# Splitting an expert's second product into three passes already in the first half, with part of the split on VectorE and GpSimd

## What is computed

```python
gate_logits = x_flat @ gate_w.T
topk_vals, topk_idx = jax.lax.top_k(gate_logits, K)          # K = 2 of E = 8
topk_w = softmax(topk_vals)
for e in range(E):
    h = gelu(x_flat @ w1[e].T + b1[e])                        # "up": 128 -> 512
    y = h @ w2[e].T + b2[e]                                   # "down": 512 -> 128
    out = out + comb[:, e:e + 1] * y
```

## Time and profile before

| | us |
|---|---|
| median of 3 runs (lowest to highest) | 195.1 (194.87 to 195.27) |
| the profiled execution | 193.53 |
| its span, first to last instruction | 191.7 |
| PE busy in it | 173.8 |
| ACT busy | 116.5 |
| DVE busy | 99.8 |
| POOL busy | 76.2 |

### The profile page before, as it was taken

How to read it: one execution, slowest core, us unless ns; L and a number is a source line. 1 busy time by engine, 2 the same in 40 slices (tenths; PEclk the granted TensorE clock), 3 DMA queues, 4 the chain that set the end, 5 groups by cost and what they waited for, 6 DMA issues and landing times.

```text
span 191.7 us, 3184 instructions
## 1 busy us (share of the span) xinstructions
PE 173.8 (91%) x1255; PEld 116.1 (61%) x1255; DVE 99.8 (52%) x171; ACT 116.5 (61%) x174; POOL 76.2 (40%) x64
## 2 busy tenths in 40 slices
PE   0698799899898999998998999899999999999991
PEld 0198667476456654445463556366666888888880
DVE  0579433878084356566000700071528979966673
ACT  3533743127626632224986498635669999999980
POOL 8304419586402020002633263328632939333222
PEclk9975999999999999999999999999999999999999
DMA  6898000000000000480000000000000086000001
GB/s 153 269 350 359 14 0 3 0 0 0 3 3 2 0 2 0 154 280 10 0 0 3 0 0 0 5 0 0 0 0 3 6 265 227 2 0 0 3 0 55
DMA packets 5647, 10.41 MB, mean 54 GB/s; under 512 B 1264, under 2 KB 1648, under 8 KB 5376
## 3 DMA queue, kind: packets, MB, share of 16 engines
q1 hardware_dynamic: 5072, 10.06, 15.3%
q10 hardware_dynamic: 560, 0.15, 0.4%
HBM read 9.65 MB, written 0.56 MB: 53 GB/s over the span
## 4 chain that ended last, share of the span: by engine, by line
PE 74%; DVE 10%; issue 5%; ACT 4%; POOL 3%; DMA 2%; another core or an unknown queue 0%; DVEq 0%; POOLq 0%; ACTq 0%
PE PS L1063 10%; PE PS L1043 8%; PE PS L1047 7%; PE PS L1044 7%; PE PS L1071 4%; PE PS L1068 4%; PE PS L1069 4%; PE PS L916 4%; DVE nmx L621 3%; PE PS L929 3%; PE PS L798 3%; PE PS L1000 2%; PE PS L818 2%; DMA convw_sb<-convw 2%; PE PS L829 2%
## 5 line engine op out<-in xcount | busy, mean ns | idle before, releaser
L469 ACT ACTIVATE room<-PS,b_sb 128x512 f32<-128x512 f32 x64 | 43.5, 686 | 32.7 <-PE PS L1047 31.8
L323 POOL TENSOR_TENSOR x_sb<-x_sb,room 128x512 f32<-128x512 f32 x15 | 22.5, 1500 | 53.0 <-DVE room L709 53.0
L700 DVE TENSOR_TENSOR Gl<-room,Gh 128x512 fp32r<-128x512 f32 x32 | 29.0, 922 | 11.1 <-ACT Gh L418 10.8
L1043 PE MATMUL PS<-x2h,w1h 128*128 128x512 f32 x64 | 32.8, 512 | 2.2 <-ACT room L469 2.2
L1063 PE MATMUL PS<-room,w_sb 128*128 128x512 f32 x64 | 32.1, 593 | 0.0
L621 DVE TENSOR_REDUCE nmx<-PS 128x4 f32<-128x1024 f32 x16 | 19.4, 1225 | 12.1 <-PE PS L929 8.3
L1047 PE MATMUL PS<-x2l,w1h 128*128 128x512 f32 x64 | 25.3, 396 | 0.0
L1044 PE MATMUL PS<-x2h,w1l 128*128 128x512 f32 x64 | 25.3, 395 | 0.0
L640 DVE RECIPROCAL att<-PS 128x256 f32<-128x256 f32 x4 | 7.0, 1756 | 34.0 <-PE PS L1016 34.0
L315 POOL TENSOR_TENSOR pairs<-probs 128x512 f32<-128x512 f32 x12 | 15.0, 1271 | 16.2 <-ACT probs L459 16.2
L1043 PEld LDWEIGHTS PS<-x2h,w1h 128*128 128x128 f32 x64 | 12.0, 188 | 14.7 <-issue 10.9
(11 more groups left out here) (114 smaller groups left out, 254.9 us busy)
## 6 DMA issues: line engine op xcount, KB each, us to landing
room<-comb_rows SPq DMA_DIRECT2D x16, 256.0 KB, 5.2
w1raw<-w SPq DMA_DIRECT2D x8, 256.0 KB, 5.9
w_sb<-w SPq DMA_DIRECT2D x2, 1024.0 KB, 10.1
x_sb<-x SPq DMA_DIRECT2D x2, 256.0 KB, 3.6
out<-x_sb SPq DMA_DIRECT2D x2, 256.0 KB, 4.2
attw_sb<-attw SPq DMA_DIRECT2D x1, 320.0 KB, 6.4
cst<-consts SPq DMA_DIRECT2D x1, 228.5 KB, 5.3
convw_sb<-convw ACTq DMA_DIRECT2D x1, 80.0 KB, 3.6
```

Source lines behind the costliest of these rows:

```text
L323: nc.gpsimd.tensor_tensor(t2[:, cols(p)], t2[:, cols(p)], part[:, s, :], ALU.add).then_inc(acc_done, 1)
L469: nc.scalar.activation(G[:, n % GR, :], PS[:, U_BANK[n % 2], :], ACT.Gelu, bias=b1_sb[:, c:c + 1])\
L700: nc.vector.tensor_tensor(Gl[:, n % GR, :], G[:, n % GR, :], Gh[:, n % GR, :].bitcast(f32), ALU.subtract)\
L1043: mm(o, w1h[e][:, ms], x2h[:, cols(p)], start=True, stop=False)
```

## The change

The downs of the first half are plain only for its first three experts (n < 12) and split from n = 12 on (`SPLIT0` = 12). The high parts of the 20 gelus n = 12 to 31 are made on VectorE; the low parts of the odd ones are made on GpSimd and those of the even ones on VectorE. The second half is split as before, high parts on ScalarE, low parts on VectorE.

The weights are split earlier: `w2h` on ScalarE at n = 0 to 7, in the order of experts 3 to 7, 0, 1, 2, and `w2l` on GpSimd for experts 3 to 6 at n = 1 to 4 and for experts 7, 0, 1, 2 at n = 26, 27, 29, 31. Memory: `w2h` takes the place of the raw first weights; `Gh`, `Gl` and four `w2l` that of the first half's attention; the other four `w2l` that of `pairs`, so the one for expert 7 waits for the last sums (`sums_done` 8).

The lags change from 3 to a pattern of 4 or 5 and 2, so that four downs are issued together at n = 16, 20 and 24 and none at the other steps from 13 to 23. The units stand at n = 11, 15, 19, 23, four steps apart. `weigh` stands one step later in the first half (visit k at n = 4k + 9). `gelu(n)` waits for the low part of n - 4 where that is split, as the buffer is free only then.

```diff
+W2_ORDER = [3, 4, 5, 6, 7, 0, 1, 2]
...
-        LAGS = [1] * 9 + [2] + [3] * (MT * VISITS - 10)
+        LAGS = [1] * 9 + [2, 3, 4, 2, 3, 4] + [5, 2, 3, 4] * 2 + [5, 2] + [3] * (MT * VISITS - 25)
...
-        WEIGH_LAG = 8
+        WEIGH_LAG = 9
...
-        SCORES, ATTENDS = {11: 4, 14: 5, 19: 6, 22: 7}, {16: 2, 24: 3}
+        SCORES, ATTENDS = {11: 4, 15: 5, 19: 6, 23: 7}, {16: 2, 24: 3}
...
-        SPLIT0 = MT * E
-        HIGH_W2 = {26: 0, 27: 1, 29: 2, 30: 3, 31: 4, 33: 5, 34: 6, 35: 7}
-        LOW_W2 = {27: 0, 28: 1, 30: 2, 31: 3, 37: 4, 39: 5, 41: 6, 43: 7}
+        SPLIT0, SECOND = 3 * MT, MT * E
+        HIGH_W2 = {n: e for n, e in enumerate(W2_ORDER)}
+        LOW_W2 = {**{n + 1: e for n, e in enumerate(W2_ORDER[:4])}, 26: 7, 27: 0, 29: 1, 31: 2}
+
+        def high_engine(n):
+            return "dve" if n < SECOND else "act"
+
+        def low_engine(n):
+            return "pool" if n < SECOND and n % 2 else "dve"
...
         def downs(n):
-            lag = [LAGS[k] - (k - 1 in SCORES) for k in (n - 1, n) if k >= 0]
-            done = [max(0, k + 1 - l) for k, l in zip((n - 1, n)[-len(lag):], lag)]
-            return range(done[0] if n else 0, done[-1])
+            return range(max(0, n - LAGS[n - 1]) if n else 0, n + 1 - LAGS[n])
...
-                if n == MT * k + WEIGH_LAG + (k == E) - (k > E):
+                if n == MT * k + WEIGH_LAG - 2 * (k > E):
...
+                if e == W2_ORDER[4]:
+                    pool.wait_ge(sums_done, 8)
...
+            def low_gelu(n):
+                pool.wait_ge(g_high["dve"], high_count(n))
+                nc.gpsimd.tensor_tensor(Gl[:, n % GR, :], G[:, n % GR, :], Gh[:, n % GR, :].bitcast(f32), ALU.subtract)\
+                    .then_inc(g_low["pool"], 1)
...
+                if n >= SPLIT0 and low_engine(n) == "pool":
+                    low_gelu(n)
...
+                if k >= SPLIT0:
+                    act.wait_ge(g_low[low_engine(k)], low_count(k))
...
+            def high_gelu(n):
+                dve.wait_ge(gelu_done, n + 1)
...
+                if n >= SPLIT0 + GR:
+                    dve.wait_ge(down_done, n - GR + 1)
+                nc.vector.tensor_copy(Gh[:, n % GR, :], G[:, n % GR, :]).then_inc(g_high["dve"], 1)
...
+                if SPLIT0 <= n < SECOND:
+                    high_gelu(n)
+                if n >= SPLIT0 and low_engine(n) == "dve":
                     low_gelu(n)
```

More of the change, by code:

```diff
@@ L69, in hybrid_program @@
         b1_sb = sb("b1_sb", [128, E * MT])
-        w1raw = [sb(f"w1raw{e}", [128, HID]) for e in range(E)]
+        with ExitStack() as early:
+            w1raw = [early.enter_context(nc.sbuf_tensor(f"w1raw{e}", [128, HID], f32)) for e in range(E)]
+        w2h = [sb(f"w2h{e}", [128, HID], f32r) for e in range(E)]
         w1h = [sb(f"w1h{e}", [128, HID], f32r) for e in range(E)]
@@ L114, in hybrid_program @@
         att = sb("att", [128, 2, TOK])
-        with ExitStack() as early:
[L117 to L128, removed]
+        kT = [sb(f"kT{g}", [128, T]) for g in range(2)]
+        qT = [sb(f"qT{g}", [128, T]) for g in range(2)]
+        other_nmx = sb("other_nmx", [128, 2, TILES, 128])
+        other_vpad = sb("other_vpad", [128, TILES, HEADS, 32])
+        shared_probs = sb("shared_probs", [128, 2, 4, 2, TOK])
+        with ExitStack() as early:
+            pairs = early.enter_context(nc.sbuf_tensor("pairs", [128, 2, 4, TOK], f32))
+        w2l = {e: sb(f"w2l{e}", [128, HID], f32r) for e in W2_ORDER[4:]}
+        with ExitStack() as early:
+            first_probs = early.enter_context(nc.sbuf_tensor("first_probs", [128, 2, 4, 2, TOK], f32))
+            first_nmx = early.enter_context(nc.sbuf_tensor("first_nmx", [128, 2, TILES, 128], f32))
+            first_vpad = early.enter_context(nc.sbuf_tensor("first_vpad", [128, TILES, HEADS, 32], f32))
         Gh = sb("Gh", [128, GR, HALF], f32r)
         Gl = sb("Gl", [128, GR, HALF], f32r)
+        w2l.update({e: sb(f"w2l{e}", [128, HID], f32r) for e in W2_ORDER[:4]})
+        nmx, vpad = (first_nmx, other_nmx), (first_vpad, other_vpad)
         PS = ctx.enter_context(nc.psum_tensor("PS", [128, 8, 512], f32))
@@ L287, in _ @@
             nc.gpsimd.memset(euler[:, :], float(np.exp(1.0))).then_inc(powers, 1)
-            nc.gpsimd.memset(vpad[:, :, :, :], 0.0).then_inc(vzero, 1)
-            nc.gpsimd.memset(nmx[:, :, :, :], 0.0).then_inc(vzero, 1)
+            for p in range(NHALF):
+                nc.gpsimd.memset(vpad[p][:, :, :, :], 0.0).then_inc(vzero, 1)
+                nc.gpsimd.memset(nmx[p][:, :, :, :], 0.0).then_inc(vzero, 1)
             for q in range(WQ):
@@ L362, in _ @@
                     low_weights2(LOW_W2[n])
-                if n >= WEIGH_LAG and n % MT == 0:
-                    k = (n - WEIGH_LAG) // MT
-                    accumulate(k, k % 2, k // E)
+                for k in range(VISITS - 2):
+                    if n == MT * k + WEIGH_LAG - (k >= E):
+                        accumulate(k, k % 2, k // E)
+                if n >= SPLIT0 and low_engine(n) == "pool":
+                    low_gelu(n)
             accumulate(VISITS - 2, 0, 1)
@@ L999, in values @@
                     for j in range(4):
-                        last = mm(PS[head_rows(j), PV_BANK[b], 0:TOK], vpad[:, 2 * b + mt, 2 * j + g, :],
-                                  probs[:, u % 4, j, mt, :], start=(g == 0 and mt == 0), stop=(g == 1 and mt == 1),
+                        last = mm(PS[head_rows(j), PV_BANK[b], 0:TOK], vpad[b // 2][:, 2 * (b % 2) + mt, 2 * j + g, :],
+                                  probs_of(u)[:, j, mt, :], start=(g == 0 and mt == 0), stop=(g == 1 and mt == 1),
                                   skip_group_check=True)
@@ L1012, in sums @@
                     pe.wait_ge(t2_ready, b)
+                    pe.wait_ge(prob_ready, 4 * b + 4)
                 for mt in range(1 if PAIRED[u] else 2):
                     for j in range(4):
[L1015 removed]
+                        addend = pairs[:, u % 2, j, :] if PAIRED[u] else probs_of(u)[:, j, mt, :]
                         last = mm(PS[head_rows(j), SUM_BANK[b], 0:TOK], ones_par[:, g, :], addend,
```

65 lines of the change are left out of this document (40 added, 25 removed).

## The result

| | before | after |
|---|---|---|
| median of the runs, us | 194.99 (194.04 to 195.27, 4 runs) | 200.26 (198.71 to 200.74, 4 runs) |
| ratio, with 95% interval | | 1.028 (1.022 to 1.034) |
| profiled execution, us | 193.53 | 200.74 |
| its span, us; mean granted clock | 191.7; 0.982 | 199.0; 0.966 |

The change costs 5.3 us. The forecast was 199.5, with a range of 194.0 to 202.5. Some executions of a kernel are slow ones, over 1.5% above its fastest: medians take them in and ratios leave them out, so the two disagree for `e3_both` and `e10_reduce_copy`, and the profiles of `e8_act24` and `e11_gate_first` are of slow ones.

A forecast was written before the change was run, and what follows sets the result against it. TensorE bounds from 150 us; earlier it also waits for gelus. With GpSimd and VectorE taking turns, +4.4 on the profiled 193.5 gave 197.9, and 1.6 for the median 199.5 us; own range 197.0 to 202.0, with other cases 194.0 to 202.5.

The forecast's parts named there:

- The mechanism and the sign: GpSimd and VectorE exclude each other by turns, making the norm's spread late; slower by 4.4 us.
- The turns: A GpSimd instruction takes 1.58 us alternating with a copy, 1.73 with a subtraction, against 1.28.
- From the spread to n = 35: up(30) starts 5.2 us late, less 0.9 by shorter downs; up(35) 4.4 late.
- The gate's transposes: TensorE's wait there stays, accumulate 6 and the exponential following low part 31: 0.
- Behind n = 36: Behind up(35) everything is as before, 1.39 us a step.
- casts do not wait for GpSimd: Nine copies in GpSimd's busy stretches save 0.3 us each: +1.7, 196.8 us; chance 0.15.
- faster, turns cost little: GpSimd goes at 1.28 us an instruction, up(35) starts at 141.8: -2.1, 193.0 us; chance 0.15.
- TensorE alone bounds: Fewer passes save 3.4 us and filled waits 3.2: -6.6, 188.5 us; chance 0.05.
- Worse: Casts of n = 13 to 15 held, a raw maximum delayed: +1.3 and +1 on top, 201.8 us; chance 0.10.

The follow-up runs named there:

- e3_both: Changed kernel with the last norm's variances and power moved ahead and w2l of experts 0, 1, 2 made at n = 33, 37, 41; 202.99 us, ratio 1.024.
- e10_reduce_copy: Changed kernel with VectorE's high parts written by a maximum over one element instead of a copy; 197.74 us, ratio 1.018.
- e8_act24: Changed kernel with high parts of n = 24 to 31 on ScalarE and their low parts all on VectorE; 197.31 us, ratio 1.011.
- e11_gate_first: `e9_all` with the second half's gate ahead of other work and the twelve high parts left on VectorE made by reduction; 193.35 us, ratio 0.995.
- e1_norm_first: Changed kernel with the last norm's variances ahead of high part 28 and their power ahead of w2l 0 and low part 27; 199.19 us, ratio 1.020.
- e5_order_only: Changed kernel with the first half's downs plain as before, keeping its lags, units and positions; 194.41 us, ratio 0.997.
- e9_all: Changed kernel, high parts from n = 24 on ScalarE, norm early, two accumulates late, w2l 0, 1, 2 at n = 29, 31, 35; 198.07 us, ratio 1.015.
- e12_order_gate: `e5_order_only` with the second half's gate ahead of weigh and low parts, its exponential one step sooner; 193.18 us, ratio 0.991.
- e4_before_memsets: Kernel before with GpSimd's two memsets cut into four of half the size; 195.0 us, ratio 1.000.

## Why the prediction was right, and where not

Two lines of VectorE in the profile after, the norm's `x2l` and a low part ahead of the gate, are read below:

```profile
143.31 1.66 DVE L698 TENSOR_TENSOR x2l<-xn,x2h 128x512 fp32r<-128x512 f32 x1
...
149.22 1.84 DVE L752 TENSOR_TENSOR Gl<-room,Gh 128x512 fp32r<-128x512 f32 x1
```

- *The mechanism and the sign* held. VectorE's high parts average 0.95 us (0.8 to 1.2 was said), the longest wait stands ahead of the spread with 3.45 (3 to 5 was said), and a step of up and split down in the first half takes 1.40 (111.73 to 113.13). `e1_norm_first` moves the norm ahead and shortens that wait to 0.46, `e8_act24` and `e10_reduce_copy` take away part of the load and shorten it to 1.80 and 2.35; `e5_order_only` takes all of the load away and the wait with it. Of GpSimd I had said over 1.5 on average and under 10 us idle from 109 to 148; it has 1.47 and 10.0.
- *The turns* were mis-sized. The five GpSimd instructions from accumulate 4 to low part 27 took 7.33 us (131.44 to 138.77), 1.47 each, where I had 8.3. All four groups together have 1.47 (30.9 us for 21), against 1.58 beside copies and 1.73 beside subtractions; why a turn costs less than the whole of the other instruction is not shown. In the burst before it the nine instructions took 14.60 (111.51 to 126.11) where I had 15.6, and that with an idle of 1.29 that I had at nothing. So the `up` behind the products of attend 3 starts at 127.69, with the 2.14 taken off 125.55, as before and not 1.1 later. The spread is +3.2 against before instead of +5.2.
- *From the spread to n = 35* the lateness was to fall from 5.2 to 4.4. It grew, from 3.2 to 3.7. From up(30) to up(35) the trace has 8.79 where I had 7.5. I had given the norm's own split nothing. Behind the spread `x2h` and `x2l` (1.66 us, before 0.69) now stand in turn with GpSimd, so `x2l` ends 4.4 us behind the spread's start (before: 2.9), and TensorE waits 0.57 for it. Counted by starts of passes that is 0.7 of the 1.3; the rest is TensorE's own work, for which 7.5 was too little. Of the low parts of this burst TensorE waits for none.
- *The gate's transposes* were the term that was wrong in kind. I wrote that the wait there "stays: 0". It rose from 0.40 to 1.81, of which 1.0 is net loss at the transposes. I had looked at GpSimd's exponential alone and not at VectorE, which has the indices and the gap behind a low part of 1.84 us, in turn with an accumulate. `e9_all` has the same fault at 2.6, and `e11_gate_first` and `e12_order_gate` remove it.
- *Behind n = 36* I had 0 and the trace has 0.4: 26 steps at 1.40 instead of 1.387. Its cause is open, but it is not of the split downs: `e5_order_only` and `e12_order_gate` have 1.40 too, and `e4_before_memsets` has 1.387. The early clock, +2.14, was in no term either; it is not of the change, as variants of the changed kernel have their first `up` at 61.84 (`e10_reduce_copy`) and 62.17 (`e5_order_only`).

So the forecast came out near for a reason that is partly luck. It was 2.0 too dear up to the spread, 1.3 too cheap from there to up(35), and 1.4 too cheap at the gate and behind; the errors nearly cancel, and the last product stands at +5.1 where +4.4 was forecast. The medians differ by 5.3. The rival "casts do not wait for GpSimd" is ruled out by `e10_reduce_copy`. The rival "faster, turns cost little" had its price of a turn about half right and its end wrong, as its queue still put `nv` behind nine instructions. "TensorE alone bounds" falls with the sign. "Worse" had a raw maximum and the casts of n = 13 to 15 held: the unit of n = 11 begins 27.4 us behind up(0) in both kernels, and up(25) 63.1 in both.

The Trainium skill (SBUF — State Buffer, Who interferes with whom) says that a VectorE copy in its two-port mode and a VectorE instruction with two SBUF inputs hold a port that GpSimd needs, and that other forms do not. The trace agrees for the copies (0.95 instead of 0.42) and for the reduction (0.68, the pairs at 1.29).

## What to carry to other kernels

Before moving elementwise work to engines that look idle, list the short instructions that a whole stage waits for (a variance, a power, a gate's gap) and put them ahead of the new work in each queue; here moving the gate alone brought the last product from 124.3 to 123.2 us (`e5_order_only` to `e12_order_gate`), and moving the norm alone brought it from 130.0 to 128.3. But a short instruction moved ahead uncovers the next wait behind it, so look at the whole queue each time. Where two engines take turns, their busy times cannot be read side by side; here most but not all of the other's time had to be added. And where an instruction is used only to copy, a slower form that takes no turns can be the faster one.
